# Attribute products on 32 rows of the array, two row groups at a time, in a graph network kernel

## The chip, the cores and the metric

The kernel is one program on one core of a Trainium2 chip. The metric is device time in microseconds (us) from the start to the end of one execution, the median of several. A profile is one further execution, taken by the hardware profiler.

## The reference, cut to what matters

There are 6250 nodes with 128 features and 200000 edges with a source, a destination and two attributes. The first layer is an edge network with batch norm over the edges:

```python
ef = concat([x[row], x[col], edge_attr]);  h = ef @ W1 + b1
h = relu(batch_norm_over_edges(h) * gamma + beta)
msgs = h @ W2 + b2
out = segment_sum(msgs, row) / (counts + 1) + x
```

After it come a layer norm, three graph convolutions (each a product with a 128x128 weight and a normalised sum over the edges) and a second layer norm.

## The kernel before, in words

The nodes are cut into B = 49 blocks of P = 128. An edge belongs to a cell: the pair of its source block and its destination block, 49 x 49 = 2401 cells, with room for 128 edges each. The program has three phases. Phase one sorts the edges into the cells and builds the 49 x 49 adjacency blocks. Phase two, the source-block pass, is the one that changes. Phase three is the three convolutions.

Phase two goes over the source blocks b. For each of the 49 cells c of a block, TensorE adds seven products of 128 x 128 x 128 in bf16 into one 128-column slice of a PSUM bank (function `hidden`):

- one attribute product (L1257): the stationary operand is `at_rows[u][:, g, :]`, the moving one `wvb[:, k, :]`;
- three products for the source node (L1261) and three for the destination node (L1263). Their stationary operand is a 0/1 matrix out of `T`, their moving operand one of three bf16 parts of the node's projected features.

The cells go in groups g of four (g = 0 to 11) and a last one of one cell (g = 12). A group has its own bank: `banks[g % 4]`, and a fifth for g = 12. The attributes of a cell fill AR = 18 rows. Before the change the four cells of a group lie one under the other: cell k of the group on rows 32k to 32k + 17 of `at_rows[u][:, g, :]`. So all four cells load the same 128 rows as stationary operand, and the moving operand `wvb[:, k, :]`, which is zero outside rows 32k to 32k + 31, picks the cell. Every product of the phase uses all 128 rows of the array.

When a group's products are done (`mm_done`), ScalarE writes relu of the bank as bf16 (L1311, waits for `mm_done` and for `sum_done` of the bank's former group, since it writes `zb`), VectorE makes the remainder (L1383, `left`, counts `z_res`), ScalarE rounds it (L1304, `middle`), VectorE makes the third part (L1388, `low`, counts `z_low`). TensorE then sums the group over its edges: one product of 128 x 128 x 384 per cell (L1277, function `sums`). In the order of TensorE's instructions, group g's `hidden` is followed by the `sums` of group g - 3. Before `hidden` of a group TensorE waits for `z_res` of the group that had the bank before it (`bank_free`), and before groups 0, 3, 6 and 9 for a quarter of `T` (`t_ready`).

VectorE makes the quarters for the next block in its own order behind groups 6, 9, 12 and 3 (L1371 makes `T` in place, L1378 makes `hotf`, the stationary operand of `sums`); behind group 4 it takes the sum of the block before (L1393). SyncE's queue loads `at_rows` (L1207, four transfers a block) and the rows of which `T` is made (L1212). Ahead of the pass, a chain of VectorE instructions ends in `wvb` (L1362 to L1366). TensorE's program has 1 block and then a loop with 16 blocks written out in its body, which runs three times.

At three other places TensorE's products do not use all 128 columns or rows: the transposes of L860 in phase one (a stationary operand of 49 columns), L1235 and L1236 (three columns, fp32) and L1240 and L1241 (three rows, fp32) before phase two.

Of the kernel before, what the change touches and what calls it, by code (L numbers as in the profile page):

```python
# [21 lines left out]
BF16 = mybir.dt.bfloat16  # L22
U16 = mybir.dt.uint16
ALU = mybir.AluOpType
# [3 lines left out]
NODES, EDGES, D, P = 6250, 200000, 128, 128  # L28
# [9 lines left out]
EP = P * COLS  # L38
NF = 10
TPB = 34  # L40
TG, HT = TPB // 2, TPB + 2
SAMP, SAMP_STEP = 98, 16
LAST_START = (-(-EDGES // SAMP_STEP) - 1) * SAMP_STEP
BW = B + 1
# [4 lines left out]
AR, GR = 18, 13  # L49
QUARTERS = ((0, 3), (3, 6), (6, 9), (9, 13))  # L50
# [477 lines left out]
def build(nc, t, out):  # L528
# [7 lines left out]
    with outer:  # L536
        def mk(ctx):
# [3 lines left out]
        sb, _ = mk(outer)  # L541
        V = nc.vector
# [5 lines left out]
        masks = sb("masks", [P, 10])  # L548
# [4 lines left out]
        S = {n: sem(n) for n in """src_in attr_in const_in weights_in xT_in dv dve_start pe_start ints_done fields_done attr_hi rec_out proj_ready p_done q_done hi res mid low  # L553
             hot_ready base_ready based orank_ready prod_ready prod_used cells_ready turned rows_ready hsd_ready hsd_used t_read
             pa_ready a_ready a_final y_ready r_ready pool_step gq_ready deg_out fits_ready pf_in q3_in phase1""".split()}
# [48 lines left out]
        with early:  # L604
            sb, _ = mk(early)
# [20 lines left out]
            with one:  # L626
# [69 lines left out]
                def group(g):  # L696
                    return range(4 * g, min(4 * g + 4, B))
# [466 lines left out]
            with two:  # L1164
# [8 lines left out]
                at_rows = [x1_free[:, 3264 + u * GR * P // 2:3264 + (u + 1) * GR * P // 2].bitcast(BF16).rearrange("p (g s) -> p g s", g=GR) for u in range(2)]  # L1173
                mom = sb("mom", [P, B, 3]); xs = sb("xs", [4, 2 * D])
                psq = [sb(f"psq{u}", [P, 7, D]) for u in range(2)]
                wvb = sb("wvb", [P, 4, D], BF16); neg_g = sb("neg_g", [P, D]); bt = [sb(f"bt{u}", [P, D]) for u in range(4)]
                nb = [sb(f"nb{u}", [P, D], BF16) for u in range(3)]
                ph = [ps(f"ph{u}", [P, 512]) for u in range(4)]
                pSum = [ps(f"pSum{u}", [P, 512]) for u in range(2)]
# [3 lines left out]
                def which(g):  # L1183
                    return 4 if g == 12 else g % 4
# [5 lines left out]
                def bank_free(eng, s, b, g):  # L1190
                    if not (isinstance(b, int) and b == 0 and (g < 4 or g == 12)):
                        eng.wait_ge(s, users(b, g))
# [7 lines left out]
                def sp_2(sp):  # L1200
                    sp.wait_ge(S["rows_set"], 1)

                    def attributes(b, u):
                        rows = arow_dram[b:b + 1] if isinstance(b, int) else arow_dram[bass.ds(b, 1)]
                        for k in range(4):
                            n = 13 if k == 0 else 12
                            sp.dma_start(at_rows[u][32 * k:32 * k + AR, 0:n, :], rows.rearrange("a f (g k) s -> k (a f) g s", k=4)[k][:, 0:n, :]).then_inc(attr_rows[u], 16)  # L1207

                    def quarter(b, k):
                        c0 = 4 * QUARTERS[k][0]  # L1210
                        rows = lrow_dram[b:b + 1] if isinstance(b, int) else lrow_dram[bass.ds(b, 1)]
                        sp.dma_start(T[k], rows[:, :, c0:c0 + QCELLS[k], :].rearrange("a f c s -> a f (c s)").to_broadcast([P, 2, QCELLS[k] * P])).then_inc(t_in[k], 16)  # L1212
                    attributes(0, 0)
                    sp.wait_ge(S["square_used"], 7)
                    for k in range(4):
                        quarter(0, k)
                    with sp.Fori(0, (B - 1) // 2) as i:
                        for h in range(2):
                            b = i * 2 + h
                            put(sp, S["mm_done"], b * 13 + 1)  # L1220
                            attributes(b + 1, 1 - h)
                            for k in range(4):
                                put(sp, S["mm_done"], b * 13 + QUARTERS[k][1])
                                quarter(b + 1, k)
# [4 lines left out]
                def pe_2(pe):  # L1229
                    pe.wait_ge(S["moments_in"], 1)  # L1230
                    pe.wait_ge(S["pf_in"], 16)
                    for i in range(7):
                        pe.wait_ge(S["squared"], i + 1)
                        for j in range(7):
                            nc.tensor.matmul(pSum[0][0:3, 0:D], mom[:, 7 * i + j, :], pf[:, 7 * i + j, :], start=i == j == 0, stop=i == j == 6)  # L1235
                            last = nc.tensor.matmul(pSum[1][0:3, 0:D], mom[:, 7 * i + j, :], psq[i % 2][:, j, :], start=i == j == 0, stop=i == j == 6)  # L1236
                        last.then_inc(S["square_used"], 1)
                    nc.tensor.matmul(st[:, 0:2 * D], ones_f[:], acc[:], start=True, stop=False)
                    pe.wait_ge(S["weighed"], 1)
                    nc.tensor.matmul(st[:, D:2 * D], ones_f[0:3, :], xs[0:3, 0:D], start=False, stop=False)  # L1240
                    nc.tensor.matmul(st[:, D:2 * D], ones_f[0:3, :], xs[0:3, D:2 * D], start=False, stop=True).then_inc(S["stats_made"], 1)  # L1241
                    pe.wait_ge(S["q3_in"], 16)
                    pe.wait_ge(S["bound_ready"], 1)

                    def hidden(b, m, u, g):

                        if g == 0:
                            pe.wait_ge(attr_rows[u], 64 * (m + 1))
                        for k, (lo, hi) in enumerate(QUARTERS):
                            if lo <= g < hi:  # L1250
                                q = k
                        if g == QUARTERS[q][0]:
                            pe.wait_ge(S["t_ready"], b * 4 + (q + 1))
                        bank_free(pe, S["z_res"], b, g)
                        bank = banks[which(g)]
                        for k, c in enumerate(group(g)):
                            nc.tensor.matmul(bank[:, k * P:(k + 1) * P], at_rows[u][:, g, :], wvb[:, k, :], start=True, stop=False)  # L1257
                            at = (c - 4 * QUARTERS[q][0]) * P
                            p_b = p3[:, b:b + 1, :, :] if isinstance(b, int) else p3[:, bass.ds(b, 1), :, :]
                            for m3 in range(3):  # L1260
                                nc.tensor.matmul(bank[:, k * P:(k + 1) * P], T[q][:, 0, at:at + P], p_b[:, :, m3, :].rearrange("p a d -> p (a d)"), start=False, stop=False)  # L1261
                            for m3 in range(3):
                                last = nc.tensor.matmul(bank[:, k * P:(k + 1) * P], T[q][:, 1, at:at + P], q3[:, c, m3, :], start=False, stop=m3 == 2)  # L1263
                        last.then_inc(S["mm_done"], 1)

                    def sums(b, u, g):
                        for k, (lo, hi) in enumerate(QUARTERS):
                            if lo <= g < hi:
                                q = k
                        if g == QUARTERS[q][0]:  # L1270
                            pe.wait_ge(S["hf_ready"], b * 4 + (q + 1))
                        if g == 0 and not (isinstance(b, int) and b < 2):
                            pe.wait_ge(S["sum_taken"], b - 1)
                        pe.wait_ge(S["z_low"], b * 13 + (g + 1))
                        for k, c in enumerate(group(g)):
                            at = c - 4 * QUARTERS[q][0]
                            last = nc.tensor.matmul(pSum[u][:, 0:3 * D], hotf[q][:, at // 2, :, at % 2], zb[which(g)][:, k, :, :].rearrange("p m d -> p (m d)"), start=c == 0, stop=c == B - 1)  # L1277
                        last.then_inc(S["sum_done"], 1)

                    def one_block(b, m, u):  # L1280
                        for g in range(13):
                            hidden(b, m, u, g)
                            if g >= 3:
                                sums(b, u, g - 3)
                            elif not (isinstance(b, int) and b == 0):
                                sums(b - 1, 1 - u, 10 + g)
                    each_block(pe, one_block, 16)
                    for g in (10, 11, 12):
                        sums(B - 1, (B - 1) % 2, g)

                def act_2(act):
# [27 lines left out]
                def dve_2(dve):  # L1319
# [42 lines left out]
                    link(V.scalar_tensor_tensor(out=bt[0][:], in0=nb[0][:], scalar=masks[:, 3:4], in1=wv[:], op0=ALU.mult, op1=ALU.add))  # L1362
                    link(V.scalar_tensor_tensor(out=bt[1][:], in0=nb[1][:], scalar=masks[:, 4:5], in1=bt[0][:], op0=ALU.mult, op1=ALU.add))
                    link(V.scalar_tensor_tensor(out=bt[0][:], in0=nb[2][:], scalar=masks[:, 5:6], in1=bt[1][:], op0=ALU.mult, op1=ALU.add))
                    for k in range(4):
                        last = V.tensor_scalar(wvb[:, k, :], bt[0][:], masks[:, 6 + k:7 + k], None, ALU.mult)  # L1366
                    last.then_inc(S["bound_ready"], 1)

                    def quarter(b, k):
                        dve.wait_ge(t_in[k], b * 16 + 16)  # L1370
# [440 lines left out]
```

## Time and profile before

| What | Value |
|---|---|
| time, median of 3 | 4371.11 us (4369.69 to 4374.78) |
| time of the profiled execution | 4368.35 us |
| its span, first to last instruction | 4366.5 us |
| mean granted TensorE clock | 0.938 of 2.4 GHz |
| phase two, from its first product at 1595.6 us to its last end at 2946.6 us | 1351 us |

"PE" is TensorE's products, "PEld" its loads of stationary operands, DVE is VectorE, ACT ScalarE, POOL GpSimd, SP SyncE; PEclk is the granted TensorE clock. A form such as "128\*49" is rows times columns of the stationary operand. Products are pipelined: one of 128 columns has a duration of some 219 ns but the next begins long before it has ended, so the distance of two starts is the price of a product in a dense row of them, not its duration. In a merged row "x3" the time is from the first start to the last end.

### The profile page before, as it was taken

The page shows a single profiled execution, that of the slowest core. Times are in us where ns is not written, and L with a number is a line of the kernel's source. Part 1 is how long each engine was busy: PE and PEld are TensorE (multiplying, and loading weights), DVE is VectorE, ACT ScalarE, POOL GpSimd, SP SyncE. Part 2 cuts the span into 40 slices and gives each one's busy share as a digit, 9 for nine tenths or more (in the row PEclk, how much of TensorE's full clock was granted, in tenths as well). Part 3 has the DMA queues.
Part 4 walks back from the last instruction along what each step waited for, and adds up shares of the span by engine and source line. Part 5 has one row for each costly group of instructions (what it writes and reads, how often), then busy time and mean ns, then how long its engine had stood idle before and what let it go on. Part 6 is the DMA issues. An engine that isn't in the chain of part 4 may idle for free.

```text
span 4366.5 us, 97953 instructions
## 1 busy us (share of the span) xinstructions
PE 3801.1 (87%) x39213; PEld 2615.8 (60%) x39213; DVE 2923.0 (67%) x4063; ACT 1251.6 (29%) x2294; POOL 583.2 (13%) x396
## 2 busy tenths in 40 slices
PE   3388888888888869999999999993499999999999
PEld 3255555555555558888888888882244444444444
DVE  5899999999999748887888888886611111111112
ACT  3133333333333325554555455551100000000000
POOL 0034444444444400000000000000000000000000
PEclk7699999999999989999999999995699999999999
DMA  5122222222222433333333333322166656656664
GB/s 189 46 76 76 75 77 63 80 71 76 76 76 76 161 75 128 129 130 117 129 129 129 121 123 130 128 99 63 56 212 195 200 190 197 195 187 203 208 208 143
DMA packets 410938, 550.57 MB, mean 126 GB/s; under 512 B 181942, under 2 KB 347546, under 8 KB 403930
## 3 DMA queue, kind: packets, MB, share of 16 engines
q1 hardware_dynamic: 404090, 540.66, 38.8%
q10 hardware_dynamic: 6624, 6.42, 0.4%
q8 instruction: 201, 3.29, 0.3%
q14 instruction: 23, 0.19, 0.0%
HBM read 437.47 MB, written 109.56 MB: 125 GB/s over the span
## 4 chain that ended last, share of the span: by engine, by line
PE 63%; DVE 28%; issue 6%; DMA 2%; ACT 1%; DVEq 1%; SPq 1%; POOL 0%; ACTq 0%; POOLq 0%
PE py L1522 27%; PE ph L1261 9%; PE ph L1263 9%; PE pSum L1277 9%; DVE prod_raw L1066 8%; DVE ring_raw L1037 6%; DVE q L1116 4%; PE ph L1257 3%; PE pbk L868 3%; DVE q L1106 1%; PE pY L828 1%; DVE rank L1133 1%; DVE q L1037 1%; DMA q_dram<-q3st 1%; DMA deg_dram<-deg_all 1%
## 5 line engine op out<-in xcount | busy, mean ns | idle before, releaser
L1522 PE MATMUL py<-ring_raw,p 128*128 128x512 bf16 (+1 forms) x3822 | 785.5, 368 | 11.2 <-DMA ring_raw<-at_dram 9.3
L1261 PE MATMUL ph<-p,prod_raw 128*128 (+1 forms) x7056 | 780.0, 219 | 5.0 <-issue 5.0
L1263 PE MATMUL ph<-q,prod_raw 128*128 128x128 bf16 x7056 | 780.4, 220 | 0.0
L1522 PEld LDWEIGHTS py<-ring_raw,p 128*128 128x128 bf16 x3822 | 362.7, 98 | 425.5 <-issue 14.1
L1383 DVE SCALAR_TENSOR_TENSOR ring_raw<-ph,x 128x512 f32<-128x512 f32 x588 | 404.8, 689 | 210.0 <-ACT x L1311 208.2
L1311 ACT ACTIVATE x<-ph 128x512 bf16<-128x512 f32 x588 | 351.3, 597 | 674.8 <-PE ph L1263 674.8
L1257 PE MATMUL ph<-wvb,x 128*128 128x128 bf16 x2352 | 515.2, 219 | 17.8 <-DVE prod_raw L1371 14.6
L868 PE MATMUL pbk<-prod_raw,q 128*128 128x392 bf16 x1666 | 373.6, 390 | 178.6 <-DVE q L1037 178.6
L1261 PEld LDWEIGHTS ph<-p,prod_raw 128*128 128x128 bf16 x7056 | 493.4, 98 | 44.5 <-issue 5.3
L1277 PE MATMUL pSum<-x,ring_raw 128*128 128x384 bf16 x2401 | 498.8, 327 | 0.3 <-DVE x L1388 0.3
L1697 DVE TENSOR_TENSOR tT<-py,dinv_row 128x512 f32<-128x512 f32 (+1 forms) x39 | 25.8, 661 | 702.2 <-PE py L1522 702.1
L1263 PEld LDWEIGHTS ph<-q,prod_raw 128*128 128x128 bf16 x7056 | 494.9, 98 | 0.0
L828 PE MATMUL pY<-p,ring_raw 128*128 128x384 bf16 x2401 | 492.2, 326 | 1.9 <-POOL ring_raw L767 1.9
L913 ACT ACTIVATE ring_raw<-pA 128x512 bf16<-128x512 f32 (+1 forms) x637 | 358.8, 570 | 258.4 <-PE pA L816 258.2
L1388 DVE TENSOR_TENSOR x<-ring_raw,x 128x512 bf16<-128x512 f32 (+1 forms) x637 | 415.1, 652 | 0.1
L868 PEld LDWEIGHTS pbk<-prod_raw,q 128*128 128x128 bf16 x1666 | 177.5, 109 | 365.7 <-issue 262.5
L1522 PE MATMUL py<-ring_raw,g 128*128 128x512 bf16 (+1 forms) x1911 | 391.1, 367 | 2.0 <-DVE dummy L1709 2.0
L1304 ACT ACTIVATE x<-ring_raw 128x512 bf16<-128x512 f32 (+1 forms) x637 | 381.2, 598 | 2.6 <-DVE ring_raw L1383 1.1
L1066 DVE TENSOR_TENSOR prod_raw<-q 128x1666 bf16<-128x1666 bf16 x392 | 376.6, 1029 | 6.4 <-PE pbk L868 6.4
L1037 DVE TENSOR_TENSOR ring_raw<-iota_lo,x 128x3584 bf16<-128x3584 bf16 x196 | 374.5, 1950 | 7.5 <-PE pX L821 7.5
L1565 ACT ACTIVATE xT<-tT,cb 128x512 f32<-128x512 f32 (+1 forms) x39 | 27.2, 697 | 1046.8 <-DVE tT L1697 1046.8
L1522 PEld LDWEIGHTS py<-ring_raw,g 128*128 128x128 bf16 x1911 | 180.9, 98 | 207.8 <-DVE dummy L1709 2.1
(263 smaller groups left out, 4690.6 us busy)
## 6 DMA issues: line engine op xcount, KB each, us to landing
ring_raw<-at_dram SPq DMA_DIRECT2D x252, 896.0 KB, 4.8
prod_raw<-lrow_dram SPq DMA_DIRECT2D x147, 768.0 KB, 4.2
at_dram<-ring_raw SPq DMA_DIRECT2D x49, 1568.0 KB, 5.6
prod_raw<-lrow_dram SPq DMA_DIRECT2D x49, 832.0 KB, 4.3
arow_dram<-x SPq DMA_DIRECT2D x147, 73.5 KB
x<-arow_dram SPq DMA_DIRECT2D x147, 54.0 KB
x<-pq_dram SPq DMA_DIRECT2D x49, 128.0 KB, 2.2
q<-q_dram SPq DMA_DIRECT2D x1, 4704.0 KB, 25.8
```

The costliest lines, as they stand in the source:

```text
L828: last = nc.tensor.matmul(pY[1 - par][:, 0:3 * D], abuf[1 - par][:, b, :], p3[:, b, :, :].rearrange("p m d -> p (m d)"), start=b == 0, sto ...
L868: last = nc.tensor.matmul(pbk[:, 0:8 * B], orank[:, i // 2, :, i % 2], prod[:, :, i // 2, :, i % 2], start=i == 0, stop=i == TPB - 1)
L1037: return V.tensor_tensor(to, iota_lo[:].unsqueeze(1).to_broadcast(dims), of.unsqueeze(2).to_broadcast(dims), ALU.is_equal)
L1066: return V.tensor_tensor(prod[:, f, :, :, :], hot_p, rec[u][:, 2 + f, :].rearrange("p (g u) -> p g u", u=2).unsqueeze(2).to_broadcast(dims ...
L1257: nc.tensor.matmul(bank[:, k * P:(k + 1) * P], at_rows[u][:, g, :], wvb[:, k, :], start=True, stop=False)
L1261: nc.tensor.matmul(bank[:, k * P:(k + 1) * P], T[q][:, 0, at:at + P], p_b[:, :, m3, :].rearrange("p a d -> p (a d)"), start=False, stop=False)
L1263: last = nc.tensor.matmul(bank[:, k * P:(k + 1) * P], T[q][:, 1, at:at + P], q3[:, c, m3, :], start=False, stop=m3 == 2)
L1277: last = nc.tensor.matmul(pSum[u][:, 0:3 * D], hotf[q][:, at // 2, :, at % 2], zb[which(g)][:, k, :, :].rearrange("p m d -> p (m d)"), sta ...
L1304: nc.scalar.activation(zb[which(g)][:, 0:w, 1, :], res[which(g)][:, 0:w, :], ACT.Copy).then_inc(S["z_mid"], 1)
L1383: V.scalar_tensor_tensor(out=res[u][:, 0:w, :], in0=banks[u][:, 0:w * P].rearrange("p (c d) -> p c d", d=D), scalar=0.0, in1=zb[u][:, 0:w, ...
L1388: V.tensor_tensor(zb[u][:, 0:w, 2, :], res[u][:, 0:w, :], zb[u][:, 0:w, 1, :], ALU.subtract).then_inc(S["z_low"], 1)
L1522: last = nc.tensor.matmul(py[par][:, 0:w], g3[c % 2][:, 7 * i + m, k, :], ring[i][:, 0:w // P, m, :], start=i == m == k == 0, stop=i == m ...
```

## The change

The four cells of a group now share their rows: group g lies on rows 32 (g mod 4) to 32 (g mod 4) + 31, its four cells side by side. The attribute product of a cell takes only these 32 rows of both operands (`at_rows[u][tile, ...]`, `wvb[tile, :]`), so that `wvb` needs one copy in place of four masked ones. TensorE's order is made of pairs of groups (0, 1), (2, 3) to (10, 11), and 12 by itself. For each k it issues the attribute product of cell k of the first group, that of cell k of the second (other rows, other bank), then the six node products of the first and the six of the second. After a pair come the `sums` of two groups, those four groups back (`h - 4`) in place of three. A block's attribute rows come in five transfers in place of four.

```diff
-                wvb = sb("wvb", [P, 4, D], BF16); ...
+                wvb = sb("wvb", [P, D], BF16); ...
...
-                        for k in range(4):
-                            n = 13 if k == 0 else 12
-                            sp.dma_start(at_rows[u][32 * k:32 * k + AR, 0:n, :], rows.rearrange("a f (g k) s -> k (a f) g s", k=4)[k][:, 0:n, :]).then_inc(attr_rows[u], 16)
+                        for j in range(4):
+                            to = at_rows[u][32 * j:32 * j + AR, 0:12, :].rearrange("p (i k) s -> p i (k s)", k=4)
+                            of = rows[:, :, 0:48, :].rearrange("a f (i j k) s -> j (a f) i (k s)", j=4, k=4)[j]
+                            sp.dma_start(to, of).then_inc(attr_rows[u], 16)
+                        sp.dma_start(at_rows[u][0:AR, 12, :], rows[:, :, 48, :].rearrange("a f s -> (a f) s")).then_inc(attr_rows[u], 16)
...
-                    def hidden(b, m, u, g):
+                    def hidden(b, m, u, first, second):
-                        if g == 0:
-                            pe.wait_ge(attr_rows[u], 64 * (m + 1))
+                        if first == 0:
+                            pe.wait_ge(attr_rows[u], 80 * (m + 1))
+                        for g in (first, second):
+                            if g is not None:
+                                if g == QUARTERS[part_of(g)][0]:
+                                    pe.wait_ge(S["t_ready"], b * 4 + (part_of(g) + 1))
+                                bank_free(pe, S["z_res"], b, g)
+                        def attributes(g, k):
+                            tile = slice(32 * (g % 4), 32 * (g % 4) + 32)
+                            nc.tensor.matmul(banks[which(g)][:, k * P:(k + 1) * P], at_rows[u][tile, 4 * (g // 4) + k, :], wvb[tile, :], start=True, stop=False)
+                        def nodes(g, k, last_cell):
...
-                            nc.tensor.matmul(bank[:, k * P:(k + 1) * P], at_rows[u][:, g, :], wvb[:, k, :], start=True, stop=False)
...
+                        for k in range(len(group(first))):
+                            attributes(first, k)
+                            if second is not None:
+                                attributes(second, k)
+                            nodes(first, k, k == len(group(first)) - 1)
+                            if second is not None:
+                                nodes(second, k, k == 3)
...
-                        for g in range(13):
-                            hidden(b, m, u, g)
-                            if g >= 3:
-                                sums(b, u, g - 3)
-                            elif not (isinstance(b, int) and b == 0):
-                                sums(b - 1, 1 - u, 10 + g)
+                        for g in range(0, 13, 2):
+                            hidden(b, m, u, g, g + 1 if g < 12 else None)
+                            for h in (g, g + 1)[:1 if g == 12 else 2]:
+                                if h >= 4:
+                                    sums(b, u, h - 4)
+                                elif not (isinstance(b, int) and b == 0):
+                                    sums(b - 1, 1 - u, 9 + h)
...
-                    for k in range(4):
-                        last = V.tensor_scalar(wvb[:, k, :], bt[0][:], masks[:, 6 + k:7 + k], None, ALU.mult)
-                    last.then_inc(S["bound_ready"], 1)
+                    V.tensor_copy(wvb[:], bt[0][:]).then_inc(S["bound_ready"], 1)
```

## Rows read from the trace of the kernel before

**Rows 1.** The page: busy time by engine; 40 slices of the span.

```profile
PE 3801.1 (87%) x39213; PEld 2615.8 (60%) x39213; DVE 2923.0 (67%) x4063; ACT 1251.6 (29%) x2294; POOL 583.2 (13%) x396
...
PE   3388888888888869999999999993499999999999
...
PEclk7699999999999989999999999995699999999999
```

**Rows 2.** Phase two, after it, before it: busy us by engine, clock, DMA share.

```profile
1595.00:2947.00 1352.00, 1339.52 (x19208) 1177.35 (x19208) 1141.03 (x1715) 681.65 (x1274) 0.00 (x0) 0.99 0.37 124
2947.00:4366.00 1419.00, 1266.67 (x6272) 627.04 (x6272) 331.39 (x805) 55.73 (x106) 0.00 (x0) 0.94 0.55 174
```

**Rows 3.** Groups by form, TensorE, phase two: count | busy us, mean ns | idle before.

```profile
L1263 PE MATMUL ph<-q,prod_raw 128*128 128x128 bf16 x7056 | 780.4, 220 | 0.0
L1261 PE MATMUL ph<-p,prod_raw 128*128 x6912 | 763.0, 219 | 5.0 <-issue 5.0
L1257 PE MATMUL ph<-wvb,x 128*128 128x128 bf16 x2352 | 515.2, 219 | 17.8 <-DVE prod_raw L1371 14.6 <-issue 3.2
L1277 PE MATMUL pSum<-x,ring_raw 128*128 128x384 bf16 x2401 | 498.8, 327 | 0.3 <-DVE x L1388 0.3
```

**Rows 4.** Timeline of TensorE, steady phase two: start us, us, what.

```profile
2199.82 0.22 PE L1257 MATMUL ph<-wvb,x 128*128 128x128 bf16 x1
2199.87 0.33 PE L1261 MATMUL ph<-p,prod_raw 128*128 x3
2200.04 0.33 PE L1263 MATMUL ph<-q,prod_raw 128*128 128x128 bf16 x3
2200.21 0.82 PE L1277 MATMUL pSum<-x,ring_raw 128*128 128x384 bf16 x4
2200.87 0.22 PE L1257 MATMUL pS<-wvb,x 128*128 128x128 bf16 x1
...
2228.06 0.22 PE L1257 MATMUL pS<-wvb,x 128*128 128x128 bf16 x1
```

**Rows 5.** Timeline of TensorE around the transposes of phase one (49 columns).

```profile
605.72 0.61 PE L852 MATMUL pbk<-q,upper 128*128 128x49 bf16 x17
606.26 0.63 PE L860 MATMUL ptr<-identb,x 128*49 128x128 bf16 x8
606.82 0.41 PE L816 MATMUL pA<-ring_raw 128*128 128x128 bf16 x4
```

**Rows 6.** The same at a later step, with products of seven columns behind it.

```profile
1022.88 0.63 PE L860 MATMUL ptr<-identb,x 128*49 128x128 bf16 x8
1023.44 0.41 PE L816 MATMUL pA<-ring_raw 128*128 128x128 bf16 x4
1023.68 0.17 PE L820 MATMUL pS<-x,ring_raw 128*128 128x7 bf16 x1
1023.71 0.17 PE L821 MATMUL pX<-x,ring_raw 128*128 128x7 bf16 x1
1023.74 0.17 PE L820 MATMUL pS<-x,ring_raw 128*128 128x7 bf16 x1
```

**Rows 7.** Timeline of TensorE, from three columns to 128, fp32.

```profile
1581.62 0.38 PE L1236 MATMUL pSum<-psq,mom 128*3 128x128 f32 x2
1581.84 0.38 PE L1235 MATMUL pSum<-prod_raw,mom 128*3 128x128 f32 x2
1582.06 0.38 PE L1236 MATMUL pSum<-psq,mom 128*3 128x128 f32 x2
1582.37 0.70 PE L1238 MATMUL st<-acc,ones_f 128*128 128x256 f32 x2
```

**Rows 8.** Timeline of TensorE in phase three, from fp32 to bf16, all 128*128.

```profile
3195.51 1.05 PE L1510 MATMUL pg<-cw,xT 128*128 128x128 f32 x8
3196.40 0.38 PE L1522 MATMUL py<-ring_raw,p 128*128 128x512 bf16 x1
```

**Rows 9.** Timeline of VectorE and ScalarE, steady phase two.

```profile
2205.97 0.60 ACT L1311 ACTIVATE x<-ph 128x512 bf16<-128x512 f32 x1 [1.42 <-PE ph L1263]
2206.47 0.62 ACT L1304 ACTIVATE x<-ring_raw 128x512 bf16<-128x512 f32 x1
2206.61 0.69 DVE L1383 SCALAR_TENSOR_TENSOR ring_raw<-ph,x 128x512 f32<-128x512 f32 x1 [0.88 <-ACT x L1311]
2207.21 0.68 DVE L1388 TENSOR_TENSOR x<-ring_raw,x 128x512 bf16<-128x512 f32 x1
```

**Rows 10.** Timeline of VectorE where a quarter is made.

```profile
2203.04 1.01 DVE L1371 TENSOR_SCALAR prod_raw<-prod_raw,pid 128x3072 bf16<-128x3072 bf16 x1
2203.97 0.95 DVE L1378 TENSOR_TENSOR ring_raw<-iota_lo,x 128x1536 bf16<-128x1536 bf16 x1
2204.84 0.68 DVE L1383 SCALAR_TENSOR_TENSOR ring_raw<-ph,x 128x512 f32<-128x512 f32 x1
```

**Rows 11.** Timeline of VectorE just ahead of phase two.

```profile
1593.65 0.87 DVE L1366 TENSOR_SCALAR wvb<-bt,masks 128x128 bf16<-128x128 f32 x4
1594.44 1.01 DVE L1371 TENSOR_SCALAR prod_raw<-prod_raw,pid 128x3072 bf16<-128x3072 bf16 x1
```

**Rows 12.** Timeline of SyncE's queue, and the page's DMA issues (KB, us to landing).

```profile
2203.88 2.37 SPq L1207 DMA_DIRECT2D x<-arow_dram  x4
...
x<-arow_dram SPq DMA_DIRECT2D x147, 54.0 KB
```

More of the change, by code:

```diff
@@ L40 @@
 TPB = 34
-TG, HT = TPB // 2, TPB + 2
+TG = TPB // 2
+HT = TPB + 2
 SAMP, SAMP_STEP = 98, 16
@@ L1175, in build @@
                 psq = [sb(f"psq{u}", [P, 7, D]) for u in range(2)]
-                wvb = sb("wvb", [P, 4, D], BF16); neg_g = sb("neg_g", [P, D]); bt = [sb(f"bt{u}", [P, D]) for u in range(4)]
+                wvb = sb("wvb", [P, D], BF16); neg_g = sb("neg_g", [P, D]); bt = [sb(f"bt{u}", [P, D]) for u in range(4)]
                 nb = [sb(f"nb{u}", [P, D], BF16) for u in range(3)]
@@ L1243, in pe_2, with part_of @@
                     pe.wait_ge(S["bound_ready"], 1)
-                    def hidden(b, m, u, g):
-                        if g == 0:
-                            pe.wait_ge(attr_rows[u], 64 * (m + 1))
[L1249 to L1256, printed above, removed]
-                            nc.tensor.matmul(bank[:, k * P:(k + 1) * P], at_rows[u][:, g, :], wvb[:, k, :], start=True, stop=False)
+                    def part_of(g):
+                        return [k for k, (lo, hi) in enumerate(QUARTERS) if lo <= g < hi][0]
+                    def hidden(b, m, u, first, second):
[10 more added lines that the diff above has]
+                        def nodes(g, k, last_cell):
+                            bank, q, c = banks[which(g)], part_of(g), 4 * g + k
                             at = (c - 4 * QUARTERS[q][0]) * P
@@ L1263, in hidden @@
                                 last = nc.tensor.matmul(bank[:, k * P:(k + 1) * P], T[q][:, 1, at:at + P], q3[:, c, m3, :], start=False, stop=m3 == 2)
-                        last.then_inc(S["mm_done"], 1)
+                            if last_cell:
+                                last.then_inc(S["mm_done"], 1)
+                        for k in range(len(group(first))):
[5 more added lines that the diff above has]
+                                nodes(second, k, k == 3)
                     def sums(b, u, g):
@@ L1280, in one_block @@
                     def one_block(b, m, u):
-                        for g in range(13):
-                            hidden(b, m, u, g)
-                            if g >= 3:
-                                sums(b, u, g - 3)
-                            elif not (isinstance(b, int) and b == 0):
-                                sums(b - 1, 1 - u, 10 + g)
+                        for g in range(0, 13, 2):
[5 more added lines that the diff above has]
+                                    sums(b - 1, 1 - u, 9 + h)
                     each_block(pe, one_block, 16)
-                    for g in (10, 11, 12):
+                    for g in (9, 10, 11, 12):
                         sums(B - 1, (B - 1) % 2, g)
```

## The prediction

> **What bounds the kernel now.** I read the page first. TensorE is at 87% of the span, and in the slices of phase two it shows 9s with PEclk 9 [rows 1]. The sum over stretches says the same more sharply: of the 1352 us of phase two TensorE's products cover 1339.5, at a clock of 0.99, so 2.4 GHz throughout but for moments; VectorE is busy 1141, ScalarE 682, the DMA engines 37% [rows 2]. By form, the four kinds of product of the phase waited 23.1 us in total, nearly all at its start and at the two turns of TensorE's loop; the sums waited for VectorE 0.3 us [rows 3]. So in steady state nothing but TensorE's own stream sets the time, and each nanosecond of it counts 1:1.
>
> The timeline prices that stream. An attribute product and the next product start 0.055 us apart, the three source products and the three destination products take 0.17 us each from start to start, four sums of 384 columns 0.66 us [rows 4]. A cell is 7 x 0.056 + 0.165 = 0.557 us, 49 cells 27.3 us; the two rows of the one-cell group, one block apart, give 2228.06 - 2200.87 = 27.19 us. 49 blocks are 1332 us; with the start and the turns of the loop that is the phase. The 2401 attribute products cost 2401 x 0.056 = 134 us of it. Loads of stationary operands are hidden: the distance of two starts does not show them.
>
> **What the change does to that stream.** It removes no product: 2401 attribute products stay, of the same 128 columns. What is new is that they use 32 rows, while the products on both sides use 128. Two things follow, of opposite sign.
>
> *The gain.* Two products on different rows and in different banks may run beside each other. In a block there are 6 pairs of groups x 4 cells = 24 such couples, and one single product (g = 12); in all 1176 couples and 49 singles. If the second of a couple cost nothing, 1176 x 0.056 = 66 us would go. The nearest row for how closely two products can start is the distance of products of seven columns, 0.03 us by the rows, 0.026 over many [rows 6]; by that the couple saves 0.03 us, 1176 x 0.03 = 35 us.
>
> *The price.* Each couple stands alone among products of full height, so the array is switched to 32 rows before it and back behind it, 1225 times each. The trace before has no switch of rows in a dense stretch, but it has three kinds of switch in columns, and none is free. Full width to 49 columns: 17 products of L852 begin at 605.72 and their last one starts about 0.61 - 0.19 = 0.42 us later, at 606.14; they are 0.026 us apart, but L860 starts at 606.26, 0.12 later: 0.09 us too late [rows 5]. Back to full width: the last of the eight transposes starts at 606.26 + 0.63 - 0.22 = 606.67, the next product at 606.82: 0.15 us where 0.056 is usual, 0.095 too late; the later step repeats it to 0.01 us (1022.88 + 0.63 - 0.22 = 1023.29, then 1023.44) [rows 5, 6]. Three columns to full width, fp32, with no wait in between: L1236's second product starts at 1582.17, L1238 at 1582.37, 0.20 us where the distance is 0.11: 0.09 too late [rows 7]. A waiting instruction or a change of type isn't what costs: from L1510 (fp32) to L1522 (bf16), both 128*128, the last start is 3195.51 + 1.05 - 0.27 = 3196.29 and the next 3196.40, the usual 0.11 [rows 8]. Behind a switch the first load isn't hidden either: the eight transposes span 0.63 - 0.22 = 0.41 us for seven distances where 7 x 0.056 = 0.39 is usual, the four of L816 0.19 for three where 0.17 is usual, 0.02 us each [rows 5].
>
> The Trainium skill bears on this in two places. TensorEngine Tiling (Array Packing), Key Properties, says that a change of tiling mode, unlike a change of tile within a mode, makes TensorE drain; it names no figure. The trace agrees for columns, with its 0.09 to 0.095 us; for rows no run here shows it yet. The other place is among the rivals.
>
> *The sum.* A switch in 0.09, a switch out 0.095, the first load behind the switch out 0.02: 0.205 us for a couple or a single. The second product of a couple lies between 0.03 us below its old price (starts 0.026 apart) and 0.02 above it (the first load behind the switch in is exposed and nothing overlaps). A couple thus costs 0.175 to 0.225 us more than before. 1176 x 0.175 + 49 x 0.205 = 216 us; 1176 x 0.225 + 10 = 275 us. I take 0.20, the middle, since the couple's two loads go to different rows and may well overlap while the first stays exposed: 235 + 10 = +245 us. For the whole switch the bounds are nothing (rows may be cut without a drain) and these rows; I take the rows, the nearest there is: the same engine, the same array, two types, both directions, always 0.09.
>
> **The rest of the change.** *Order.* With `sums` four groups back in place of three, `zb` is free later: ScalarE's relu of group g waits for the sums of g - 4, which now stand behind the pair. Count from the end of a pair's products: sums end at 0.66 and 1.32 us. The first relu starts at some 0.9 (a product's end lags its columns by 0.16), `left` at 1.5, `low` at 2.1, then where a quarter is due L1371 and L1378 take 0.93 + 0.87 us, and the second `left` starts at 4.6 and ends at 5.3 [rows 9, 10]. The pair that needs this bank starts at 1.32 + 8 x 0.39 + 1.32 = 5.76. So there is 0.5 us of room at the tightest place (groups 6 and 7), and with slower TensorE more: cost nothing; without it, each 0.1 us short would be 49 x 0.1 = 5 us. *Ends.* One product of VectorE for four ahead of the phase: 0.87 us becomes about 0.28, it delays `T` as well, so -0.6 us [rows 11]. Behind the last pair four sums in place of three wait on the chain of relu, `left`, `middle`, `low`: about +0.6 us. They cancel. *Transfers.* A fifth transfer a block on SyncE's queue: 2.37 / 4 = 0.6 us of issue; the rows are wanted 20 us later and the next quarter is issued two pairs later, so it is hidden; its cover gone, it is 49 x 0.6 = 29 us at the very most [rows 12]. *Semaphores and loop.* A pair has its waits in front of its first product instead of in front of each group; the instructions of TensorE's loop body are as many as before, so its turns cost what they did.
>
> The profiled execution took 4368.35 us, 1.85 beyond its span; 4368.35 + 245 = 4613. The median is 2.8 us above that execution, so I predict 4616 us.
>
> **The rivals.** 1. *Rows switch without a drain, couples overlap.* Faster. For it: all three kinds of switch in the trace are of columns (L1240's three rows come after a wait and tell nothing), and cutting rows leaves the way into the array as it is. [...] It gives -35 us by the distance of 0.026, 66 at most: 4305 to 4336. The pair between would then end 4 x 0.056 = 0.2 us sooner, which leaves 0.3 of the room of 0.5 us above. The Trainium skill, TensorE: Matmul & The Clock Gate, part 3, speaks for it: matmuls on different row groups start about 4 ns apart; by that figure, as an estimate, 1176 x 0.052 = 61 us would go, 4310. No run here shows it yet. 2. *Neither drain nor overlap:* the stream keeps 0.056 per product, 4371. 3. *A cheaper switch:* in one direction alone, or half as long: 0.1 us a couple, 4371 + 120 = 4490, between 4390 and 4540. 4. *The order binds:* the loads of both products of a couple, or the bank waits, cost more than the rows say, up to 0.3 us a couple, 4371 + 353 = 4724. If in addition TensorE's clock fell to 1.2 GHz in the stalls, it would go further; in phase one it stays at 0.93 with TensorE busy 8 tenths [rows 1], and here no stall is over 0.2 us, so I give that almost nothing.
>
> **How the numbers follow.** Switches cost as the column switches do: 0.70, 4587 to 4646 by the bounds. Cheaper switch 0.07; dearer 0.03. No change 0.04. Overlap without drain 0.16. A change of under 0.2% (9 us) can't be told from none. So faster 0.16, same 0.05, slower 0.79. The likeliest gives 4616. The range leaves out the faster case and the dearest and takes in the rest: 4355 to 4680; the likeliest case's own range is 4570 to 4665.
>
> **What would show it.** Phase two some 245 us longer (1595 us), all else as before. Distance from the last node product to the attribute product 0.15 us and from the couple to the next product 0.15, the couple's two starts 0.03 to 0.08 apart. VectorE's idle time before L1383, which waits for ScalarE, larger, and no new wait of TensorE for VectorE. I am wrong if the first of these distances is 0.056: then rows switch for nothing, and phase two is up to 66 us shorter.

## The result and the profile after

The changed kernel takes 4567.87 us (median of 4, 4564.22 to 4571.23) against 4371.76 us before (median of 4): ratio 1.0448, 95% interval 1.043 to 1.0466. It is 196 us slower; forecast were 245 us, 4616 us, within 4355 to 4680. Its profiled execution took 4564.22 us, its span is 4562.4 us.

First the page of the changed kernel: busy time by engine and two rows of the 40 slices. Then the stretches: phase two and what follows.

```profile
PE 4003.8 (88%) x39213; PEld 2578.2 (57%) x39213; DVE 2922.2 (64%) x4060; ACT 1222.5 (27%) x2294; POOL 582.0 (13%) x396
...
PE   3488888888888699999999999996479999999999
...
PEclk7699999999999899999999999997589999999999
```

```profile
1595.00:3142.00 1547.00, 1534.64 (x19208) 1135.41 (x19208) 1140.95 (x1716) 652.49 (x1274) 0.00 (x0) 0.99 0.31 108
3142.00:4562.00 1420.00, 1269.56 (x6272) 629.43 (x6272) 331.80 (x805) 55.73 (x106) 0.00 (x0) 0.93 0.55 174
```

Against [rows 2] phase two has grown from 1352 to 1547 us with the same 19208 products and the same clock of 0.99; what follows it is 1420 where it was 1419. All 195 us are in phase two. VectorE has the same 1141 us of work in it. TensorE's busy time rose with the phase, 1339.5 to 1534.6, although it does the same products: each has a record some 0.22 us long, so a start that comes 0.1 or 0.15 us after the one before it still falls inside that one's record and shows no idle time. So the busy row can't show where the time went; distances of starts can. Next, the forms and waits of TensorE in that stretch.

```profile
L1272 PE MATMUL ph<-q,prod_raw 128*128 128x128 bf16 x7056 | 781.4, 220 | 7.1 <-issue 7.1
L1270 PE MATMUL ph<-p,prod_raw 128*128 x6912 | 776.4, 221 | 0.0
L1294 PE MATMUL pSum<-x,ring_raw 128*128 128x384 bf16 x2401 | 451.3, 326 | 0.5 <-DVE x L1404 0.5
L1263 PE MATMUL ph<-wvb,x 32*128 32x128 bf16 x2352 | 269.8, 226 | 14.0 <-DVE prod_raw L1387 11.0 <-DVE ring_raw L1399 3.0
```

TensorE waited 21.6 us, no more than the 23.1 of [rows 3]; L1263's records cover 270 us where L1257's covered 515, since the two of a couple now cover the same stretch. The timeline of TensorE in steady state shows the couples (columns as in [rows 4]):

```profile
2248.57 0.33 PE L1270 MATMUL ph<-p,prod_raw 128*128 x3
2248.73 0.33 PE L1272 MATMUL ph<-q,prod_raw 128*128 128x128 bf16 x3
2249.00 0.23 PE L1263 MATMUL ph<-wvb,x 32*128 32x128 bf16 x2
2249.16 0.34 PE L1270 MATMUL ph<-p,prod_raw 128*128 x3
2249.34 0.33 PE L1272 MATMUL ph<-q,prod_raw 128*128 128x128 bf16 x3
```

Where three products follow without a break the next row starts 0.17 later; from L1272 to L1263 it is 0.27, and the two L1263 end 0.23 us after the first began, which is hardly more than one product's 0.226: they run side by side. From the first of them to L1270 it is 0.16, where one distance is 0.056. Next the loads of the stationary operands, behind the sums:

```profile
2251.77 0.10 PEld L1294 LDWEIGHTS pSum<-x,ring_raw 128*128 128x128 bf16 x1
2252.18 0.10 PEld L1263 LDWEIGHTS ph<-wvb,x 32*128 32x128 bf16 x2 [0.32 <-issue]
2252.34 0.17 PEld L1270 LDWEIGHTS ph<-p,prod_raw 128*128 128x128 bf16 x3
```

Elsewhere in the phase a load begins 0.002 us (median) behind the start of the product before it, 0.054 us ahead of its own product where products of 128 columns follow each other. The load of L1263 begins at 2252.18, 0.25 us after the start of the last sum (2251.93 in the timeline), and its product starts 0.004 us after it (median): the load isn't brought forward over a switch, and neither is the load of L1270 at 2252.34.

Taken from every start of phase two in this trace, the medians are:

| Distance of two starts, us | before | after | count after |
|---|---|---|---|
| last destination product to attribute product | 0.056 | 0.152 | 884 |
| last sum to attribute product | 0.165 | 0.258 | 340 |
| attribute product to the second of its couple | - | 0.003 | 1176 |
| attribute product to the first source product | 0.056 | 0.158 | 1225 |
| first to second source product, behind attribute products | 0.056 | 0.066 | 1225 |

The sum of these: in 0.095 (0.096 behind node products, 0.093 behind sums), out 0.102, the late second start 0.010, 1225 times, +254 us; second of a couple 0.056 - 0.003, 1176 times, -62 us. That is some +191 us; measured are 196, and 194.3 in phase two by first start and last end (1351.0 to 1545.3).

### The profile page after: what moved, and what is told of

Read it like the earlier page. It is cut to its first block, busy times and chain, and to the rows that moved or that the text cites. A ratio compares the mean times of both kernels' runs of the same rounds, so it can differ in the third digit from the quotient of the medians.

```text
span 4562.4 us, 98100 instructions
## 1 busy us (share of the span) xinstructions
PE 4003.8 (88%) x39213; PEld 2578.2 (57%) x39213; DVE 2922.2 (64%) x4060; ACT 1222.5 (27%) x2294; POOL 582.0 (13%) x396
## 2 busy tenths in 40 slices
DMA packets 379627, 550.57 MB, mean 121 GB/s; under 512 B 140047, under 2 KB 316235, under 8 KB 372619
## 4 chain that ended last, share of the span: by engine, by line
PE 64%; DVE 26%; issue 5%; DMA 2%; ACT 1%; DVEq 1%; SPq 1%; POOL 0%; ACTq 0%; POOLq 0%
PE py L1538 26%; PE ph L1270 11%; PE ph L1272 9%; PE pSum L1294 9%; DVE prod_raw L1067 7%; DVE ring_raw L1038 6%; PE ph L1263 4%; DVE q L1117 4%; PE pbk L869 3%; DVE q L1107 1%; DVE q L1038 1%; PE pY L829 1%; DVE rank L1134 1%; DMA q_dram<-q3st 1%; DMA deg_dram<-deg_all 1%
## 5 line engine op out<-in xcount | busy, mean ns | idle before, releaser
L1270 PE MATMUL ph<-p,prod_raw 128*128 (+1 forms) x7056 | 793.7, 221 | 0.0
L1272 PE MATMUL ph<-q,prod_raw 128*128 128x128 bf16 x7056 | 781.4, 220 | 7.1 <-issue 7.1
L1272 PEld LDWEIGHTS ph<-q,prod_raw 128*128 128x128 bf16 x7056 | 495.7, 98 | 7.4 <-issue 7.4
L1270 PEld LDWEIGHTS ph<-p,prod_raw 128*128 128x128 bf16 x7056 | 448.8, 98 | 78.6
L1294 PE MATMUL pSum<-x,ring_raw 128*128 128x384 bf16 x2401 | 451.3, 326 | 0.5 <-DVE x L1404 0.5
L1294 PEld LDWEIGHTS pSum<-x,ring_raw 128*128 128x128 bf16 x2401 | 220.9, 98 | 115.9 <-DVE x L1404 1.0
```

## The experiments

Each kernel was timed with runs of the kernel before on the same chip; ratios and differences to "before" are to those. A visit is one stay in the 32 rows: a switch in, the attribute products that stand there together, a switch out. The changed kernel makes 25 visits a block, 24 for couples and one for the single product, 1225 in all.

### Attribute products alone

```diff
                         for k in range(len(group(first))):
                             attributes(first, k)
-                            if second is not None:
-                                attributes(second, k)
                             nodes(first, k, k == len(group(first)) - 1)
                             if second is not None:
+                                attributes(second, k)
                                 nodes(second, k, k == 3)
```

> Each cell's 32-row attribute product stands alone, right before its own six node products; pairs of groups, sums and transfers as in the changed kernel. Theory A, the price is per switch between 32 and 128 rows (0.095 us in, 0.102 out, 0.011 for the next load, all read from the changed kernel's trace): 2401 visits in place of 1225, nothing runs beside anything, so 2401 x 0.208 = 499 us over the kernel before, 4871 us. Theory B, a product of 32 rows is slow by itself (the 196 us spread over 2401 products): as many products as before, so 4568 us.

Measured 4880.12 us, ratio 1.1172 (1.1153 to 1.119): +511 us where theory A said +499 and B +199. Timeline of TensorE in this run:

```profile
2300.43 0.33 PE L1272 MATMUL ph<-q,prod_raw 128*128 128x128 bf16 x3
2300.69 0.23 PE L1263 MATMUL ph<-wvb,x 32*128 32x128 bf16 x1
2300.85 0.34 PE L1270 MATMUL ph<-p,prod_raw 128*128 x3
```

The distances are those of the couples, 0.26 and 0.16, now around every single product; the medians are 0.152 in, 0.158 out and 0.066 for the start after that. Twice the visits, and 2.6 times the loss, since nothing is gained beside. B is out. Most of the 12 us over A lie at the start of the phase: from 1598 to 1620 us the granted clock is 0.50, that is 1.2 GHz, where the kernel before has 0.83 from 1595 to 1610 us. By these two stretches 22 x 0.50 - 15 x 0.17 = 8 us more are lost to the clock, an estimate.

### All attribute products of a pair first

```diff
                         for k in range(len(group(first))):
                             attributes(first, k)
                             if second is not None:
                                 attributes(second, k)
-                            nodes(first, k, ...)
+                        for k in range(len(group(first))):
+                            nodes(first, k, ...)
...
-    ... wvb[tile, :], start=True, stop=False)
+    ... wvb[tile, :], start=k == 0, stop=False)
...
-    ... start=False, stop=m3 == 2)
+    ... start=False, stop=last_cell and m3 == 2)
```

> The eight attribute products of a pair of groups all stand ahead of its 48 node products (start only at a bank's first product, stop only at its last); order, rows and banks as in the changed kernel. Theory A, price per switch: 294 + 49 visits to 32 rows in place of 1225. A visit of four couples takes 0.151 + 3 x 0.056 + 0.003 + 0.158 + 0.011 = 0.491 us from the last product before to the first behind, where nine distances of 0.056 = 0.504 us stood in the kernel before: -4 us for all; 49 singles x 0.208 = +10: 4378 us. Theory B, price per product or per couple: 4568 us.

Measured 4378.73 us, ratio 1.0024 (1.0015 to 1.0034): +10 us over its own runs of before, forecast +6. One visit for eight products in the timeline:

```profile
2253.34 0.49 PE L1295 MATMUL pSum<-x,ring_raw 128*128 128x384 bf16 x2
2253.76 0.40 PE L1263 MATMUL ph<-wvb,x 32*128 32x128 bf16 x8
2254.09 0.34 PE L1270 MATMUL ph<-p,prod_raw 128*128 x3
```

Eight products from 2253.76 to the next start at 2254.09 take 0.33 us: 4 x 0.056 = 0.22, the price of four products for eight, and the rest is the switch. Same products, same rows, same banks, same order of groups: 186 of the 196 us are gone by going 343 times to 32 rows instead of 1225.

### The order alone

The changed kernel with full-height attribute products, the old layout, the four masked copies and the four transfers:

```diff
-  nc.tensor.matmul(..., at_rows[u][tile, 4 * (g // 4) + k, :], wvb[tile, :], start=True, stop=False)
+  nc.tensor.matmul(..., at_rows[u][:, g, :], wvb[:, k, :], start=True, stop=False)
```

> The changed order alone: groups in pairs, sums four groups back, but attribute products over all 128 rows with the layout, the four masked copies and the four transfers of the kernel before. Theory A, switches cost all of it: 4372 us, within 5. Theory C, part of the 196 us is the order (relu waits for sums that stand behind the pair, bank waits in front of a pair): anything over 4380, with idle time of TensorE before the first product of a pair.

Measured 4372.63 us, ratio 1.001 (1.0 to 1.0019): 4 us over its runs of before, within the 5 that were allowed. The pairs, the sums four groups back and the waits in front of a pair cost 0 to 8 us. The relu does wait for the sums now, as reasoned: in the changed kernel's waits ScalarE stands 600 us for them, and 478 us in this run, and TensorE doesn't feel it: the line below is the changed kernel's (us, times, longest).

```profile
ACT x L1329 <- PE pSum L1294: 600.5, 197, 3.4
```

### The couple on the same rows

```diff
-                            tile = slice(32 * (g % 4), 32 * (g % 4) + 32)
+                            tile = slice(32 * (g // 2 * 2 % 4), 32 * (g // 2 * 2 % 4) + 32)
```

This kernel leaves out the second group's own attributes; number and shapes of the products are those of the changed kernel.

> As the changed kernel, but the second attribute product of a couple takes the same 32 rows as the first (it reads the first group's attributes, so the values are those of other cells). Theory A with overlap between row groups (second start 0.003 us behind the first): without other rows the second costs its 0.056, 1176 x 0.053 = +62 us over the changed kernel, 4630 us. Rival: two products in the 32-row mode start together whatever their rows are, for instance because the second needs no drain: 4568 us.

Measured 4623.51 us, ratio 1.0583 (1.0565 to 1.0601), +255 us over before, 59 more than the changed kernel's +196; forecast 62. The timeline:

```profile
2249.94 0.33 PE L1272 MATMUL ph<-q,prod_raw 128*128 128x128 bf16 x3
2250.20 0.28 PE L1263 MATMUL ph<-wvb,x 32*128 32x128 bf16 x2
2250.41 0.34 PE L1270 MATMUL ph<-p,prod_raw 128*128 x3
```

The couple now takes 0.28 us to its end in place of 0.23: its starts are 0.067 us apart by the median, 0.003 in the changed kernel, and from the second to L1270 it is 0.147. So different rows are what lets the second product run beside the first. This run is also close to what my prediction had priced: +255 us where it had +245.

### 64 rows in place of 32

```diff
-                            tile = slice(32 * (g % 4), 32 * (g % 4) + 32)
+                            tile = slice(64 * (g % 4 // 2), 64 * (g % 4 // 2) + 64)
...
-    at_rows[u][tile, ...], wvb[tile, :]
+    at_rows[u][tile, ...], wvb[tile, g % 4, :]
```

> As the changed kernel, but an attribute product takes 64 rows (those of its own group and of its neighbour, the four masked copies of wvb pick its own). A couple's two products then have the same rows. Theory A, any change of height costs the same: 1225 x (0.095 + 0.102) + 1176 x 0.011 = 254 us over the kernel before, 4623 us. Rival: the price belongs to the 32-row mode or grows with the cut (half as many cuts, half the price): 4500 us or less.

Measured 4627.78 us, ratio 1.0586 (1.0568 to 1.0603): +257 us, forecast +254.

```profile
2253.86 0.33 PE L1272 MATMUL ph<-q,prod_raw 128*128 128x128 bf16 x3
2254.12 0.28 PE L1263 MATMUL ph<-wvb,x 64*128 64x128 bf16 x2
2254.34 0.34 PE L1270 MATMUL ph<-p,prod_raw 128*128 x3
```

Half the height costs what a quarter costs on the same rows: 0.151 in, 0.067 from first to second, 0.148 out. For both heights tried it is the change that is paid, at the same price.

### Sets of three groups

What follows from this: visit the 32 rows rarely, and put as many different row groups into a visit as there are banks. Four visits a block instead of 25:

```diff
-                        for g in range(0, 13, 2):
-                            hidden(b, m, u, g, g + 1 if g < 12 else None)
+                        for gs in ((0, 1, 2), (3, 4, 5), (6, 7, 8), (9, 10, 11, 12)):
+                            hidden(b, m, u, gs)
...
+                        for k in range(4):
+                            for g in gs:
+                                if k < len(group(g)):
+                                    attributes(g, k)
+                        for g in gs:
+                            for k in range(len(group(g))):
+                                nodes(g, k, k == len(group(g)) - 1)
+                            if g >= 3:
+                                sums(b, u, g - 3)
+                            elif not (isinstance(b, int) and b == 0):
+                                sums(b - 1, 1 - u, 10 + g)
```

with start and stop as above (one accumulation for a whole bank).

> Groups in sets (0,1,2), (3,4,5), (6,7,8), (9,10,11,12): all attribute products of a set first, cell by cell over its three or four row groups and banks, then each group's node products followed by the sums of the group three back, as in the kernel before. Theory A (price per switch, products on different rows nearly free): 4 visits a block. A visit of three groups is 0.151 + 3 x 0.056 + 0.006 + 0.158 + 0.011 = 0.494 us where 13 x 0.056 = 0.728 stood, the last one 0.494 where 0.784 stood: 147 x 0.234 + 49 x 0.290 = 48.6 us less than before, 4321 us. Rival D: a set needs its last bank 2.7 us after that bank's products ended, and where VectorE makes a quarter of T in between, its `left` ends some 4.5 us after them; TensorE then waits in front of a set, up to 4 x 49 x 0.5 = 98 us in all, 4420 us, slower than before.

Measured 4341.57 us, ratio 0.9933 (0.9916 to 0.9949). Faster than before, but 20 us short of theory A. TensorE waits in small pieces, mostly inside the record of the product before, so that the profile lists no such wait. Here is one; first TensorE, then VectorE in this run:

```profile
2266.61 0.33 PE L1283 MATMUL pS<-p,prod_raw 128*128 x3
2266.77 0.33 PE L1285 MATMUL pS<-q,prod_raw 128*128 128x128 bf16 x3
2267.13 0.83 PE L1262 MATMUL pSum<-x,ring_raw 128*128 128x384 bf16 x4
```

```profile
2263.99 1.01 DVE L1385 TENSOR_SCALAR prod_raw<-prod_raw,pid 128x3072 bf16<-128x3072 bf16 x1
2264.92 0.95 DVE L1392 TENSOR_TENSOR ring_raw<-iota_lo,x 128x1536 bf16<-128x1536 bf16 x1
2265.79 0.68 DVE L1397 SCALAR_TENSOR_TENSOR ring_raw<-ph,x 128x512 f32<-128x512 f32 x1
2266.39 0.68 DVE L1402 TENSOR_TENSOR x<-ring_raw,x 128x512 bf16<-128x512 f32 x1
```

The sums of group 9 (L1262 at 2267.13) would start at 2266.94, 0.17 behind L1285, and start when `low` of group 9 (L1402, 2266.39 + 0.68 = 2267.07) has ended. VectorE was at a quarter of T (L1385, L1392) ahead of it. Over the phase the distances before the sums are 9 us too long (some 50 times 0.18) and those before a set 5 us. Rival D had named the waits before a set, those 5 us; the larger part stands before the sums, which it had not named, for the same reason, a quarter of T in VectorE's way. Both together are far below its 98 us.

### The quarters later

```diff
-                            if g == 3 and not (isinstance(b, int) and b == 0):
-                                quarter(b, 3)
+                            if g in (2, 5) and not (isinstance(b, int) and b == 0):
+                                quarter(b, 2 if g == 2 else 3)
...
-                            if g in (6, 9, 12) and not last:
-                                quarter(b + 1, (g - 6) // 3)
+                            if g in (8, 11) and not last:
+                                quarter(b + 1, (g - 8) // 3)
```

> As the sets of three, and VectorE makes its quarters of T and hotf behind groups 8, 11, 2 and 5 in place of 6, 9, 12 and 3, that is behind the `left` for which the next set waits. Theory A: 4321 us, with no idle time of TensorE in front of a set. Rival D: it is faster than the run with the quarters where they were, by what that one waits for VectorE; if both give 4321, the room was enough there too.

Measured 4323.7 us, ratio 0.9889 (0.9873 to 0.9906): 47 us faster than before, 244 faster than the changed kernel; forecast 4321. Moving the quarters gave back 18 of the 20 us, so VectorE's order was the cause of the shortfall. Timeline and stretch of this run:

```profile
2254.56 0.82 PE L1262 MATMUL pSum<-x,ring_raw 128*128 128x384 bf16 x4
2255.32 0.23 PE L1276 MATMUL ph<-wvb,x 32*128 32x128 bf16 x3
2255.32 0.23 PE L1276 MATMUL pS<-wvb,x 32*128 32x128 bf16 x1
2255.38 0.33 PE L1276 MATMUL ph<-wvb,x 32*128 32x128 bf16 x9
2255.65 0.34 PE L1283 MATMUL ph<-p,prod_raw 128*128 x3
```

```profile
1598.00:2901.00 1303.00, 1290.90 (x19208) 1075.26 (x19208) 1132.87 (x1714) 680.01 (x1274) 0.00 (x0) 0.99 0.37 129
```

The thirteen attribute products of the last set, on four row groups, and the switch out fit between 2255.32 and 2255.65; one after the other the products alone would take 13 x 0.056 = 0.73 us. Phase two is 1303 us, 49 less than [rows 2].

### The control: the same order at full height

The same sets and late quarters, but attribute products over all 128 rows as in the third experiment.

> The control of the fastest version so far: the same sets of three groups, the same late quarters, all attribute products of a set first, but each over all 128 rows with the layout and the masked copies of the kernel before. Theory A, the gain of 47 us is the overlap of products on different rows less four visits a block: without both, 4371 us. Rival: the order and the late quarters gave part of it: under 4360 us.

Measured 4370.45 us, ratio 1.0002 (0.9992 to 1.0011). The order and the late quarters give nothing by themselves, within 5 us; the 47 us come from the overlap on different rows, less four visits a block.

## Why the prediction was right, point by point

The direction, the main cost and the stated range held, but the size was 49 us off: 196 us in place of 245. The time lies 2 us below the likeliest case's own range (4570 to 4665) and 19 below its bounds (4587 to 4646), towards the rival of a cheaper switch (4390 to 4540). That it lies well inside 4355 to 4680 is owed to the width of that range, which was drawn to take in nearly all rivals.

*What bounds the kernel: right.* Each part of a microsecond in TensorE's stream came out in the time: the distances add up to 191 of 196 us, and phase three did not move.

*A switch costs as the column switches do: right.* In 0.09 by [rows 5], 0.095 measured; out 0.095 and 0.02 for the load behind it, 0.115 together, 0.102 + 0.010 = 0.112 measured. The Trainium skill's rule that a change of tiling mode drains TensorE (TensorEngine Tiling (Array Packing), Key Properties) speaks for such a cost. The traces agree for rows too, with 0.09 to 0.10 us each way for 32 and for 64 rows.

*The second product of a couple: the mis-sized term.* The prediction put it between 0.03 us below and 0.02 above its old price, and took -0.005. It is -0.053: the couple's starts are 0.003 us apart. The lower bound came from products of seven columns on the full array, 0.026 apart; that is a row of products on the same rows, and two on different rows start closer. 1176 x 0.048 = 56 us is more than the whole miss of 49 us. The other 7, which give back, are 2 to 3 of the switches (0.207 for 0.205, 1225 times) and up to 4 of the order (below), none of it clear of noise. The run on the same rows gave 4623.51, next to the 4616 of the sum. The sign named for this step, starts 0.03 to 0.08 us apart, failed; the signs of the two switches, 0.15 us each, came true, and phase two is 1545 us long where 1595 was named.

The Trainium skill has a figure for this term (TensorE: Matmul & The Clock Gate, part 3): matmuls on different row groups start some 4 ns apart. The trace agrees, with 3 ns. By that figure, as an estimate, the sum would have been 1176 x (0.205 - 0.052) + 10 = 190 us, 4561. The prediction used it only for the rival without a drain, as if overlap and drain shut each other out. They hold at the same time.

*The order costs nothing: right*, 4 us at the edge of what can be told (1.0 to 1.0019). ScalarE's wait for the sums appeared, VectorE's for ScalarE before `left` grew from 208 to 404 us as named, and both stayed off TensorE's path. *Ends and transfers: no contradiction.* VectorE's four instructions of 0.87 us became one of 0.23, packets under 512 bytes fell from 181942 to 140047, and no stretch shows either; they weren't tested by themselves, but the second experiment has both and is 10 us over before in all.

*Rivals.* Faster without a drain: refuted by the first distance, 0.152 and not 0.056, as the prediction's last paragraph asked; its other half, that couples overlap, was true. No change: out. Cheaper switch: out, since both directions cost the full 0.09 to 0.10. A dearer one: out by the time. The clock stayed at 0.99 in phase two.

## What to carry to other kernels

Small products on part of the array's rows pay at both ends when products of full height stand around them: here 0.21 us a visit, nearly the time of four products of 128 columns. A visit pays only when enough stands in it, on different row groups: by the medians from the last start before it to the second start behind it, two products lost 0.155 us against full height, eight in couples broke even (0.01 won), and twelve on three row groups won 0.23. So look in the trace for any switch of shape, price it by the distance of starts and not by busy time, and count visits before counting products; to gather products into one visit, a bank's accumulation was opened once and closed once for four cells.

## What the runs showed of the hardware that was not expected

Two products on different 32-row groups with different banks start 3 ns apart, and twelve on three row groups start in four bursts, so that with the switch out they take 0.332 us where twelve of full height take 0.668 (medians of 145 sets, the last two experiments). On the same rows the second of a couple starts 67 ns behind the first, 11 ns more than the usual 56.

The overlap itself costs nothing beyond these 3 ns. The way out takes 0.158 us behind an overlapped couple, and the same 0.158 behind a product that stands alone (all 2401 of the first experiment); it takes 0.147 behind a couple on the same rows and 0.146 or 0.147 behind eight and more. So the start that follows the first product or burst of a visit is 10 or 11 ns late, once: in a longer visit that is the next attribute product, in a short one the way out. Back at full height the second start is late in the same way, 66 ns in the median of the 1225 cases. Why it is so no run shows.
